# Values and output projection made once for two images, and two of the nine reductions replaced by additions on GpSimd

## The reference, cut to what matters

```
xdw    = depthwise 3x3 convolution of x, plus dw_b
om     = xdw @ om_w + om_b                      # per group and tap: offset x, offset y, mask
value  = (x @ vp_w + vp_b).reshape(n, h, w, G=8, GC=8)
sampled[tap] = bilinear sample of value at (base + tap + offset)
out    = einsum('nhwgkc,nhwgk->nhwgc', sampled, mask) @ op_w      # sum over the 9 taps
x      = x + out
```

## Time and profile before

| | us |
|---|---|
| median of 3 runs | 484.69 (483.13 to 488.61) |
| the profiled execution, its own time | 484.25 |
| its span, first to last instruction | 482.4 |

### The profile page before, as it was taken

How to read it: one execution, slowest core, us unless ns; L and a number is a source line. 1 busy time by engine, 2 the same in 40 slices (tenths; PEclk the granted TensorE clock), 3 DMA queues, 4 the chain that set the end, 5 groups by cost and what they waited for, 6 DMA issues and landing times. The chain is left out here.

```text
span 482.4 us, 10750 instructions
## 1 busy us (share of the span) xinstructions
PE 422.5 (88%) x3788; PEld 239.8 (50%) x3788; DVE 329.4 (68%) x724; ACT 264.9 (55%) x580; POOL 141.0 (29%) x172
## 2 busy tenths in 40 slices
PE   0456999998999999999999835898999999999995
PEld 0333435444354443534433224676777777677673
DVE  2301598785987879778688934767686968768653
ACT  1555366463664646556452034457768576766752
POOL 2132242222422233322330025322332323233323
PEclk9999999999999999999999985579999999999998
DMA  7039368395684848738397041000000000000000
GB/s 245 0 77 211 107 151 223 71 216 130 148 209 94 229 111 182 209 83 225 90 203 187 1 194 67 0 2 1 1 2 12 1 2 2 12 1 2 11 2 12
DMA packets 28412, 44.95 MB, mean 93 GB/s; under 512 B 6864, under 2 KB 11088, under 8 KB 27984
## 3 DMA queue, kind: packets, MB, share of 16 engines
q1 hardware_dynamic: 28368, 44.38, 37.0%
HBM read 6.10 MB, written 0.52 MB: 14 GB/s over the span
## 5 line engine op out<-in xcount | busy, mean ns | idle before, releaser
L568 DVE TENSOR_TENSOR prod<-ps_t,a_rep 128x1024 f32<-128x1024 f32 x128 | 152.2, 1218 | 58.9 <-PE ps_t L304 58.0
L288 PEld LDWEIGHTS ps_m<-om_r,sel 128*128 128x128 f32 x216 | 35.1, 203 | 88.5 <-ACT mask L430 32.9
L304 PE MATMUL ps_t<-b,vt 32*128 32x512 f32 x512 | 74.9, 655 | 1.9 <-DVE prod L568 1.9
L641 POOL TENSOR_TENSOR a<-a,mask 128x512 f32<-128x512 f32 (+1 forms) x40 | 46.7, 1168 | 97.3 <-ACT a L451 97.3
L324 PE MATMUL ps_d<-prod,keep 128*32 128x512 f32 x512 | 68.5, 607 | 2.2 <-DVE prod L568 1.9
L288 PE MATMUL ps_m<-om_r,sel 128*128 128x256 f32 x216 | 59.4, 356 | 9.4 <-ACT mask L430 3.2
L1095 POOL TENSOR_TENSOR total<-total,share 128x256 f32<-128x256 f32 x56 | 40.9, 730 | 87.4 <-DVE share L989 87.0
L973 DVE TENSOR_TENSOR hidden<-ps_h,gated 128x256 f32<-128x256 f32 x128 | 51.3, 414 | 3.9 <-ACT gated L1188 2.4
L1188 ACT ACTIVATE gated<-ps_h 128x256 f32<-128x256 f32 x128 | 47.8, 387 | 7.9 <-PE ps_h L1308 1.4
L1308 PE MATMUL ps_h<-xf,w_h 128*128 128x256 f32 x128 | 43.9, 343 | 2.0 <-ACT gated L1188 2.0
L1182 ACT ACTIVATE factor<-ps_yf 128x256 f32<-128x256 f32 x64 | 24.6, 385 | 37.9 <-PE ps_yf L1343 37.9
(11 more groups left out here) (134 smaller groups left out, 670.1 us busy)
## 6 DMA issues: line engine op xcount, KB each, us to landing
a_rep<-a SPq DMA_DIRECT2D x128, 256.0 KB, 4.8
a_rep<-a SPq DMA_DIRECT2D x32, 128.0 KB
w_f<-in_w SPq DMA_DIRECT2D x2, 1024.0 KB, 5.8
start<-in_start SPq DMA_DIRECT2D x1, 1344.0 KB, 6.8
x_turned<-in_x_turned SPq DMA_DIRECT2D x1, 512.0 KB, 3.7
t_tok<-in_x SPq DMA_DIRECT2D x1, 512.0 KB, 8.7
w<-in_w SPq DMA_DIRECT2D x1, 512.0 KB, 7.7
select_f<-in_select SPq DMA_DIRECT2D x1, 512.0 KB, 8.4
```

The costliest lines, as they stand in the source:

```text
L288: mm = pe.matmul(ps_m[:, s * PIX:(s + 1) * PIX], sel[:, which, :], om_r[:, q, :], start=True, stop=True)
L304: mm = pe.matmul(out, vt[par][r, v % 2, :, :, :].rearrange("p j y c -> p (j y c)"), b[par][r, pair_taps(v // 2), :].rearrange("p t x -> p ...
L568: dve.tensor_tensor(p[:, :, :], t[:, :, :], a_rep[par][:, ms, pair_taps(v // 2), :].rearrange("p m t x -> p m (t x)"), ALU.mult).then_inc( ...
L641: pool.tensor_tensor(v, v, mask[(PAIRS * par + k) % 2][:, 0:wide, :], ALU.mult).then_inc(a_done, 1)
```

## The change: what it does

1. **Reduction.** POOL adds the product of batch 0 to that of batch 2, and of batch 4 to that of batch 6 (`add_up`, two instructions of 128 x 1024 f32 each, in place in SBUF). PE reduces seven batches, in the order 1, 3, 2, 5, 7, 8, 6; those of 8 and 6 lie in the next image's batches 0 and 1. Batches 3 and 7 carry no reduce.
2. **Ring** `prod` of nine pairs instead of four. What frees a pair is the reduce that read it, or POOL's addition (`let_go`).
3. **Jobs.** `values` is made once for both images of a slab, in odd images (32 columns in a matmul instead of 16). `output` and `residual` are made once for two images, in even images: `output` is the sixth job and runs behind the reduce of batch 1, `residual` comes behind weight 6. Seventeen jobs an image, none in the second place of batch 3. Even images have no v, odd ones no out.
4. ACT's `copy_d` stands behind both halves of the offsets and ahead of all `copy_rep`.
5. The weights `om_w` come by a DMA of their own; `start` and `x_turned` lie in the space of `a_rep[1]`, whose first fill waits until they have been read.

```diff
-TRING, PROD, LAG = 3, 4, 1
+TRING, PROD, LAG = 3, 9, 2
-        JOBS = [("om", 0), ("om", 1), ("v", 0)] + [("rep", r) for r in range(len(REPS))]
-        JOBS.insert(2 * LAG + 1, ("out", 0))
-        RESIDUAL_AT = 2 * LAG + 1
+        OM, REP = [("om", 0), ("om", 1)], [("rep", r) for r in range(len(REPS))]
+        JOBS = [OM + REP[0:3] + [("out", 0)] + REP[3:], OM + [("v", 0)] + REP]
+        JOBS_AT = [s for s in range(2 * BATCHES) if s != 7]
+        SUMS = {0: (8, True), 1: (6, True), 2: (1, False), 4: (3, False), 5: (2, False), 6: (5, False), 8: (7, False)}
+        ORDER = [1, 3, 2, 5, 7, 8, 6]
+        ADDED = {0: 0, 4: 1}
+        RESIDUAL_AT = 6
+        def let_go(w, i):
+            before, last = (i, w - PROD) if w >= PROD else (i - 1, WPI + w - PROD)
+            v, h = divmod(last, 2)
+            if v in ADDED:
+                return summed, 4 * before + 2 * ADDED[v] + h + 1
+            return reduced, len(ORDER) * before + ORDER.index(v) + 1
...
             def output(slab, free_sem, free):
-                pe.wait_ge(d_copied, i + 1)
+                pe.wait_ge(d_copied, 2 * slab + 2)
                 pe.wait_ge(free_sem, free)
+                for k in range(2):
...
             def job(s, i, par, slab, made):
+                    if before[0] == "v":
+                        replicate(r, n, v_done, slab + 1)
+                    elif before[0] == "out":
+                        replicate(r, n, *(freed("rep", r - 1, n) if isinstance(i, int) and i == 0 else (t_done, slab)))
...
             def image(i, par, slab, made):          # PE
                 for v in range(BATCHES):
                     sample(v, i, par)
-                    job(2 * v, i, par, slab, made)
-                    if v >= LAG:
-                        reduce(v - LAG, i, par)
-                    elif not first_image:
-                        reduce(BATCHES + v - LAG, i - 1, 1 - par)
-                    job(2 * v + 1, i, par, slab, made)
+                    job(JOBS_AT.index(2 * v), i, par, slab, made)
+                    if v in SUMS:
+                        w, last = SUMS[v]
+                        if not last:
+                            reduce(w, i, par)
+                        elif not first_image:
+                            reduce(w, i - 1, 1 - par)
+                    if 2 * v + 1 in JOBS_AT:
+                        job(JOBS_AT.index(2 * v + 1), i, par, slab, made)
...
             def image(i, par, slab, copied, made):  # ACT
-                if LAG == 1 and last is not None:
-                    copy_d(last)
-                if made:
                     copy_offsets(1, n)
                     high_offsets(1, n)
+                if not (isinstance(i, int) and i == 0):
+                    copy_d(i - 1, 1 - par, slab - 1 if par == 0 else slab)
                 if made:
-                    reps(n, npar, slab)
+                    reps(n, npar, copied)
...
                 for w in range(WPI):                # DVE
                     weight(w, i, par)
-                    if made and w == 2:
-                        v_out(i + 1)
-                    if w == RESIDUAL_AT and not (isinstance(i, int) and i == 0):
-                        residual(i - 1)
+                    if par and made and w == 2:
+                        v_out(slab)
+                    if not par and w == RESIDUAL_AT and not (isinstance(i, int) and i == 0):
+                        residual(slab - 1)
...
+            def add_up(v, i, par):                  # POOL
+                for h in range(2):
+                    pool.wait_ge(weighted, WPI * i + 2 * v + 4 + h + 1)
+                    first, second = product(2 * v + h, par), product(2 * v + 4 + h, par)
+                    pool.tensor_tensor(second[:, :, :], second[:, :, :], first[:, :, :], ALU.add).then_inc(summed, 1)
+
+            def image(i, par, slab, made):
+                n, npar = i + 1, 1 - par
+                if made:
+                    low_offsets(0, n)
+                    low_offsets(1, n)
+                    tables(n, npar, slab)
+                    masked(0, n, npar)
+                add_up(0, i, par)
+                if made:
+                    for k in range(1, PAIRS):
+                        masked(k, n, npar)
+                add_up(4, i, par)
```

More of the change, by code:

```diff
@@ L110, in conv_stage @@
         kernel_at = keep[:, at["kernel_at"]]
[L111 to L115, removed]
+        om_w = sb("om_w", [P, QUADS, P])
         sel = sb("sel", [P, SELS, P], F32R)
         om_bias = sb("om_bias", [P, QUADS])
-        x_turned = sb("x_turned", [P, SLABS, H, W])
         xpad = sb("xpad", [P, SLABS, H + 2, W + 2])
@@ L140, in conv_stage @@
         prod = [sb(f"prod{i}", [P, 2, BANK]) for i in range(PROD)]
-        d_sb = sb("d_sb", [P, BANK])
+        early = a_rep[1][:, :, :, :].rearrange("p m t x -> p (m t x)")
+        ahead = dict(zip(START, columns(START)))
+        start = early[:, 0:START_COLS]
+        sel_f = start[:, ahead["sel"]]
+        grid_f = start[:, ahead["grid"]]
+        x_turned = early[:, START_COLS:START_COLS + SLABS * PIX].rearrange("p (s y x) -> p s y x", s=SLABS, y=H)
+        d_sb = [sb(f"d_sb{i}", [P, BANK]) for i in range(2)]
         ps_t = [ctx.enter_context(nc.psum_tensor(f"ps_t{i}", [P, 2, BANK], F32)) for i in range(TRING)]
@@ L216, in fill @@
                     sp.wait_ge(weighted, used)
+                if isinstance(n, int) and n == 1:
+                    sp.wait_ge(xn_ready, SLABS)
+                    sp.wait_ge(sel_ready, 2)
                 for k in range(PAIRS):
@@ L252, in offsets, with values @@
                 mm.then_inc(om_ps, 1)
-            def values(n, slab, par):
+            def values(n, slab):
                 pe.wait_ge(om_copied, 2 * n + 2)
@@ L374, in _ @@
             offsets(1, 0, 0, 0)
-            values(0, 0, 0)
+            values(0, 0)
             pe.wait_ge(sel_ready, 1)
@@ L385, in _ @@
             image(IMAGES - 1, 1, SLABS, False)
-            for v in range(BATCHES - LAG, BATCHES):
-                reduce(v, IMAGES - 1, 1)
-            output(IMAGES - 1, t_done, IMAGES - 1)
+            reduce(8, IMAGES - 1, 1)
+            reduce(6, IMAGES - 1, 1)
+            output(SLABS - 1, t_done, SLABS - 1)
         @block.scalar
@@ L451, in hat, with copy_d @@
                     act.activation(v, v, ACT.Relu, bias=1.0, scale=-1.0).then_inc(done, 1)
[L453 to L457, removed]
+            def copy_d(i, par, slab):
+                act.wait_ge(reduced, len(ORDER) * (i + 1))
+                if positive(slab):
+                    act.wait_ge(out_ps, slab)
+                act.activation(d_sb[par][:, :], ps_d[:, :], ACT.Copy).then_inc(d_copied, 1)
             def reps(n, npar, slab):
@@ L467, in reps, with image @@
                 hat(len(REPS) - 1, n, npar)
-            def image(i, par, slab, made):
+            def image(i, par, slab, copied, made):
                 n, npar = i + 1, 1 - par
@@ L473, in image @@
                     high_offsets(0, n)
-                last = None if isinstance(i, int) and i == 0 else i - 1
-                if LAG == 1 and last is not None:
-                    copy_d(last)
-                if made:
                     copy_offsets(1, n)
                     high_offsets(1, n)
-                if LAG == 2 and last is not None:
-                    copy_d(last)
+                if not (isinstance(i, int) and i == 0):
+                    copy_d(i - 1, 1 - par, slab - 1 if par == 0 else slab)
                 if made:
-                    reps(n, npar, slab)
+                    reps(n, npar, copied)
             values_in(0)
@@ L496, in _ @@
             reps(0, 0, None)
-            image(0, 0, 1, True)
-            image(1, 1, None, True)
+            image(0, 0, 0, 1, True)
+            image(1, 1, 0, None, True)
             with act.Fori(1, IMAGES // 2 - 1) as it:
[L500 to L504, removed]
+                image(2 * it, 0, it, it + 1, True)
+                image(2 * it + 1, 1, it, None, True)
+            image(IMAGES - 2, 0, SLABS - 1, None, True)
+            image(IMAGES - 1, 1, SLABS - 1, None, False)
+            copy_d(IMAGES - 1, 1, SLABS - 1)
         @block.vector
@@ L617, in low_offsets @@
                     pool.wait_ge(a_done, PAIRS * n)
+                if half == 0 and positive(4 * (n - 1)):
+                    pool.wait_ge(summed, 4 * (n - 1))
                 pool.wait_ge(om_high, 2 * n + half + 1)
@@ L641, in masked @@
                 pool.tensor_tensor(v, v, mask[(PAIRS * par + k) % 2][:, 0:wide, :], ALU.mult).then_inc(a_done, 1)
-            def image(n, par):
-                low_offsets(0, n)
-                low_offsets(1, n)
-                tables(n, par)
-                for k in range(PAIRS):
-                    masked(k, n, par)
-            image(0, 0)
-            image(1, 1)
-            image(2, 0)
+            def add_up(v, i, par):
+                for h in range(2):
```

(16 more changed lines are left out.)

118 lines of the change are left out of this document (62 added, 56 removed).

## The result

The changed kernel takes 496.0 us (median of 4 runs, 494.8 to 497.3) against 484.2 before (median of 4 runs): ratio 1.0234, 95% interval 1.0172 to 1.0296. It is slower, by twice what was forecast (11.8 us for 5.9), and inside the range.

What follows compares the result with a forecast made beforehand. PE was taken as the bound, without idle time in steady state, DVE close behind. Savings in odd images against waits in even ones and a longer end summed to +5.9 on 484.25, forecast as 490.0 us, range 478 to 497.

Steps and rivals of the forecast that it cites:

- start: Ahead of the first sample: values and v_out of the first two images add 0.3 us.
- image 0: First image: neither Wait A nor Wait B, and no reduces to save at its start; -0.4 us.
- image 7 and the end: Last image: S(1) waits for POOL's last addition, no out in batch 1, later reduce, out and residual; together +2.7 us.
- PE's work without stalls: PE's summed steps per image after the change: 26.8 us even, 26.3 odd, against about 29.1 before.
- Wait A: Even images, ahead of rep 1: PE idles 1.35 us because ACT does copy_d before copying rep 0.
- Wait B: Even images, ahead of rep 3: PE idles 1.8 us for the residual, queued on DVE behind weight 6.
- The loop: Each sample needs a weight that needs the sample before: a batch takes at least 2.55 us, against 2.93 before.
- Wait C: End of even images: S(8) waits 1.0 us for weight 14, then R(7) 0.5 us for weight 15.
- The clock: PE's clock was read as standing at full, 1.00 (2.4 GHz); the sum has no term for it.
- The lock: Port shared by DVE and POOL: a tap behind an addition stands still until it ends, up to 2.4 us.
- the second: Rival: POOL's second addition takes the port before tap 1, weight 6 starts 2.1 us later; 496 us, chance 0.2.
- The first rival: Waits overlap or hide better, PE stays the bound, an image pair falls toward 53.1 us; 476 us, chance 0.13.

Runs made afterwards that it cites:

- e4: The changed kernel with eight zero-weight matmuls more between S(3) and rep 3 in images 2, 4 and 6; 491.0 us.
- e9: The kernel before with values for two images in one job of odd images, and output behind the first rep in even images; 478.2 us.
- e2: The changed kernel with copy_d behind the copy of rep 0 instead of ahead of it, in even images only; 489.4 us.
- e5: The changed kernel with the residual behind weight 5 and tap step 1 instead of behind weight 6; 489.7 us.
- e7: The changed kernel without POOL's additions: PE reduces all nine batches, one batch behind the samples; 489.4 us.
- e3: The changed kernel with the last three tap steps behind weights 12, 13, 14 instead of 13, 14, 16; 492.6 us.
- e1: The changed kernel with the residual behind weight 5 instead of weight 6, ahead of tap 1; 496.8 us.
- e6: The changed kernel with the edits of e2, e3 and e5 together; 481.9 us.
- e8: e7 with copy_d between the two halves of the offsets and the residual behind weight 5 and tap 1; 478.3 us.

## Why the prediction came out as it did

The direction held, and the mechanism in part: PE's work falls and its idle time grows by more. The time was inside the range, 6 us above the forecast. The parts of the sum against the profiled executions, in us (what is measured from image 7 on is the rest of the span):

| | forecast | measured |
|---|---|---|
| start | +0.3 | +0.3 |
| image 0 | -0.4 | +1.4 |
| images 1, 3, 5 | -2.7 | -0.4 |
| images 2 and 4 | +4.2 | +4.4 |
| image 6 | +1.8 | +2.8 |
| image 7 and the end | +2.7 | +2.6 |
| sum | +5.9 | +11.1 |

That images 2 and 4 agree is luck. Two half-clock stretches (3.0) are not in the forecast; the idle 1.87 of image 2 in the kernel before hid part of them, and the even image without the clock was drawn too long (31.5; e4 has 31.0). Point by point:

- *PE's work without stalls, 26.8 and 26.3.* Image 5 has 26.25 busy at full clock; image 4, less the 1.46 of the clock, 27.0. Values were priced at 1.6, between 1.38 and 1.91. In image 5 they take 1.13 (208.85 to 209.98), in images 1 and 3 of the same execution 1.08 and 1.61 (0.25 of it idle), in e9 1.34 to 1.57. The lower bound was wrong, and no single price holds; what sets it is open.
- *Wait A, 1.35.* 1.29; e2 removes it by the one edit that the argument names, and image 4 is 1.3 shorter.
- *Wait B, 1.8.* 1.65. Of this 0.8 was called B's own; e5 against e4 gives 0.3. The loop takes back the rest, 0.67 ahead of S(4) and 0.37 ahead of S(5), near the 1.0 that was given to it.
- *Wait C, 1.0 and 0.5.* 0.97 in three pieces, and the largest, 0.55, is another wait: batch 7 has no reduce between its two reps, and the second stands until ACT has copied the first. DVE's part is 0.42. In odd images S(4) waits 0.9 for 1.0, and in place of S(8)'s 0.7 stands the same 0.55.
- *The clock.* The first term that failed: it isn't in the sum. I wrote that the clock stands at full and took it for given while adding 3 us of idle time to the image. It costs 1.46 in image 4 and 1.5 in each of images 2 and 6 (4.5 together), by e4.
- *Image 0.* Forecast 0.4 shorter, it is 1.4 longer. Its steps come to full speed at about 60.7 us, before the change at 56.3; in e7, with R(0) in batch 1 again, they do so at 56.2, and the image takes 32.0 instead of 34.1. Of these 2.1 us the slow steps have 1.6, and most of the rest is a wait of S(5) for its weight that e7 doesn't have. Whether the missing reduce delays the full speed is argued, since e7 also takes the additions from POOL.
- *The lock.* I priced additions at 2.38 (2.40) and the port as a port that stands still until POOL is through; both right. Tap 1 fitted into its cover, as drawn. The second term that failed is tap 8. The prediction gave four later taps 0.1 to 0.3 each for masked products and tap 8 nothing for an addition, though it had the last additions run on into the next image. Tap 8 met the second one and lost 2.2, and I had not followed who waits for the last tap: om 0 of the next image (wait D, 1.13 to 1.22 in images 1, 3, 5). e3 shows it.
- *Image 7 and the end, +2.7.* +2.6.

Of the rivals, the second named the lock and its number, 496, was hit; but not by its mechanism. In the change tap 1 got the port between the two additions (1.44), and the pair of additions took 4.90 instead of 4.70. The lock did decide where a tap came while the second addition ran: D, and e1. The first rival, PE stays the bound, is refuted as far as this order goes. With the three waits mended (e6) the kernel is faster than before, but slower than without the additions (e8).

Where the expected gain went, then, of three parts. The values for two images are the gain that is real: 1.1 to 1.3 us a pair (e9). The output for two images gives PE nothing and brings B with it, and at the end an output of twice the length. The additions take 2 us an image off PE, and where they stand they cost more: 6.6 us on the whole as ordered (the change against e7, which still has B and half of A), the clock's part in it included, and 3.6 us with the waits mended (e6 against e8). Between e6 and e8 the loss lies in image 0 (34.2 and 31.7) and in image 7 up to its output (27.3 and 25.4).

What stays open is from what point idle time costs the clock. In the profiled executions it fell in images 2, 4 and 6 of the change, of e2 and of e3, in images 2 and 4 of e1, and in image 6 of e7 but not in its image 4, which has the same wait of 1.65. What the other executions did is known only by their mean clock. The kernel before varies too, from 482.3 us to 488.6. Its executions of over 487 us in the experiments have a mean clock of 0.950 to 0.953, the others of 0.955 to 0.962; none of the slow ones was profiled.

## What to carry to other kernels

When work is taken off an engine that is full, lay the remaining steps on a time line with the queues of the other engines, and look for the first instruction that stands behind something later than before; here that found A and B to within 0.2 us. Then follow each instruction that gets slower to whoever reads its result last, also into the next iteration (D). Count what idle time does to the clock: a gap of 1.65 us cost nearly as much again behind it, and a few matmuls of zeros in the gap gave that back. And an idle time in a trace is not what its removal gives: taking out B's 1.65 us gave 0.3, the clock apart, because the next limit stood right behind it.

## What the runs showed of the hardware

- The granted clock of TensorE fell from 1.00 to 0.50 (2.4 to 1.2 GHz) in image 4 of the change after idle times of 1.29 and 1.65 us with short output matmuls between them; no single idle time was longer than 1.65. With 1.49 us of zero-weight matmuls in the second gap it stayed at 1.00 (e4). With only the first gap, and 0.67 and 0.37 in place of the second (e5), it stayed too. With only the second it fell in e2; in e7, with 0.65 us idle ahead of it, it fell in one image of three.
- A DVE instruction with both inputs in SBUF and a POOL addition exclude each other: the tap steps took 1.44, 2.60 and 2.65 us instead of 0.47. The last two ended 0.29 us after the addition they had met, as those of the earlier trace rows ended 0.27 and 0.28 after a product. DVE's weights, which have one input in PSUM, kept 1.21 to 1.23 beside the same additions. Where a tap step was waiting when the first of two additions ended, it went first (1.44, pair 4.90).
- Sixty-four fp32 matmuls of 32 columns, each with weights of its own, took from 1.08 to 1.61 us (images 1, 3 and 5 of the change; e9 lies between), and sixty-four of 16 columns 1.34 to 1.39 (images 1, 3, 4, 5 and 6 before): twice the columns cost at most 0.3 us more and sometimes nothing.
